# VectorE's expert additions and low halves put ahead of its other work in each slot of a MetaFormer block

## What is computed

```python
x = x + _L0_conv_ref(_ln_c(x), xl, qkv_w, proj_w, proj_b)   # super-token attention
t = _to_tokens(x)
t = t + _L0_ffn_ref(_ln_t(t), gate_w, gate_b, w1, b1, w2, b2)

# the first branch: 7 by 7 cells of 8 by 8 pixels, one super token each
aff = softmax(einsum('bnpc,bnck->bnpk', pix, sf9) * scale)   # pixel to 9 nearby cells
sft = fold3(einsum('bnpc,bnpk->bnck', pix, aff)) / aff_sum
q, k, v = split(qkv_w @ sft)                                 # 8 heads of 12
out = proj_w @ attention(q, k, v) + proj_b
pix_out = einsum('bnck,bnpk->bncp', unfold3(out), aff)

# the second branch: 4 experts, the best 2 of a softmax gate weigh the sum
h = gelu(einsum('bsd,edh->ebsh', x, w1) + b1)                # 96 -> 384
y = einsum('ebsh,ehd->ebsd', h, w2) + b2                     # 384 -> 96
out = einsum('bse,ebsd->bsd', masked, y)
```

## Time and profile before

| | |
|---|---|
| median of 3 runs | 509.77 us (508.06 to 514.8) |
| profiled execution | 509.76 us |
| its span, first to last instruction | 508.0 us |
| mean granted TensorE clock | 0.945 |
| busy share of the span: PE, DVE, ACT, POOL | 94%, 80%, 68%, 30% |
| PE line that starts each slot (L1345) | 100 times, from 81.1 to 501.7 us |

### The profile page before, as it was taken

How to read it: one execution, slowest core, us unless ns; L and a number is a source line. 1 busy time by engine, 2 the same in 40 slices (tenths; PEclk the granted TensorE clock), 3 DMA queues, 4 the chain that set the end, 5 groups by cost and what they waited for, 6 DMA issues and landing times.

```text
span 508.0 us, 14090 instructions
## 1 busy us (share of the span) xinstructions
PE 479.8 (94%) x5770; PEld 347.1 (68%) x5770; DVE 405.3 (80%) x1084; ACT 346.3 (68%) x333; POOL 154.8 (30%) x289
## 2 busy tenths in 40 slices
PE   9799879999899999899899999899899979999996
PEld 5797757776567777676566877676666657666665
DVE  6563875988899688988899687778799867888886
ACT  1026227578876849578877749669878938989883
POOL 3224012132870532131861541130343812112000
PEclk9759759999999999999899999899999989999999
DMA  8844015210120214210120210120220210223100
GB/s 237 286 141 144 1 33 132 43 34 17 32 56 19 48 34 112 50 32 17 33 56 18 48 34 19 32 48 17 32 57 17 49 33 21 47 48 79 26 17 20
DMA packets 55629, 28.18 MB, mean 55 GB/s; under 512 B 53534, under 2 KB 53670, under 8 KB 55173
## 3 DMA queue, kind: packets, MB, share of 16 engines
q1 hardware_dynamic: 54450, 24.99, 21.2%
q10 hardware_dynamic: 1114, 2.29, 1.4%
HBM read 12.33 MB, written 4.82 MB: 34 GB/s over the span
## 4 chain that ended last, share of the span: by engine, by line
PE 72%; DVE 8%; ACT 8%; issue 4%; DMA 4%; POOL 3%; SPq 0%; ACTq 0%; DVEq 0%; POOLq 0%
PE ps L1360 21%; PE ps L1388 16%; PE ps L1393 7%; PE ps L1380 5%; PE ps L1364 5%; PE ps L1223 4%; PE ps L1210 4%; ACT h L729 4%; DMA xt<-xtok 3%; ACT hh L737 2%; DVE xt L1068 2%; PE ps L1190 2%; PE ps L1300 2%; PE ps L1234 1%; PE ps L1345 1%
## 5 line engine op out<-in xcount | busy, mean ns | idle before, releaser
L729 ACT ACTIVATE h<-ps 128x1536 f32<-128x1536 f32 (+1 forms) x100 | 142.6, 1426 | 80.0 <-PE ps L1364 79.8
L1052 DVE TENSOR_TENSOR hl<-h,hh 128x1536 f16<-128x1536 f32 (+1 forms) x91 | 161.4, 1773 | 14.7 <-issue 13.7
L737 ACT CAST hh<-h 128x1536 f16<-128x1536 f32 (+1 forms) x91 | 133.3, 1465 | 2.9
L1068 DVE SCALAR_TENSOR_TENSOR xt<-ps,gl,xt 128x96 f32<-128x96 f32 (+1 forms) x400 | 99.8, 309 | 31.1 <-PE ps L1393 24.0
L510 POOL TENSOR_TENSOR x<-xs,x 128x384 f16<-128x384 f32 (+1 forms) x28 | 39.7, 1419 | 254.4 <-ACT x L693 254.4
L1388 PE MATMUL ps<-w_hi,hh 128*128 128x96 f16 x1092 | 107.2, 209 | 0.0
L1388 PE MATMUL ps<-w_lo,hh 128*128 128x96 f16 x1092 | 106.6, 209 | 0.0
L1388 PEld LDWEIGHTS ps<-w_hi,hh 128*128 128x128 f16 x1092 | 95.1, 100 | 10.0 <-issue 5.7
L1388 PEld LDWEIGHTS ps<-w_lo,hh 128*128 128x128 f16 x1092 | 96.2, 99 | 0.0
L1360 PE MATMUL ps<-xhl,w_a 128*128 128x512 f16 (+1 forms) x336 | 84.1, 360 | 3.1 <-DMA xhl<-x 3.1
L1360 PE MATMUL ps<-xhl,w_b 128*128 128x512 f16 (+1 forms) x336 | 82.8, 356 | 0.0
(11 more groups left out here) (168 smaller groups left out, 554.9 us busy)
## 6 DMA issues: line engine op xcount, KB each, us to landing
xch<-x SPq DMA_DIRECT2D x4, 1176.0 KB, 7.6
out<-xt SPq DMA_DIRECT2D x24, 192.0 KB, 2.2
xt<-xtok SPq DMA_DIRECT2D x4, 663.0 KB, 13.0
xt<-xtok SPq DMA_DIRECT2D x4, 612.0 KB, 11.3
h<-w ACTq DMA_DIRECT2D x2, 570.0 KB
h<-w ACTq DMA_DIRECT2D x1, 576.0 KB
xhl<-x SPq DMA_TRANSPOSE x28, 3.7
wqkv_sb<-wqkv ACTq DMA_DIRECT2D x1, 228.0 KB
```

What stands on the lines that cost most here:

```text
L729: act.activation(h32[:, i % 3, :, 0:width(i)], z, ACT.Gelu, scale=1.0 / WS).then_inc(S["h_ready"], 1)
L737: act.copy(hh[:, i % 3, :, 0:width(i)], h32[:, i % 3, :, 0:width(i)]).then_inc(S["hh_ready"], 1)
L1052: dve.tensor_tensor(hl[:, i % 2, :, 0:n], h32[:, i % 3, :, 0:n], hh[:, i % 3, :, 0:n], ALU.subtract).then_inc(S["hl_ready"], 1)
L1068: ins = dve.scalar_tensor_tensor(out=xt[0:n, b, t, 0:C], in0=ps[0:n, sum_bank(i), j * C:(j + 1) * C], scalar=gl[0:n, b % 2, t, e:e + 1], i ...
```

## The change

In each slot DVE now does the low part, the second side read and `add_expert(i)` first, and its normalising, statistics, sums and gates after it. Around that, numbers of slots are shifted:
- `NORMAL` becomes {2: 2, 5: 3, 8: 4, 10: 5, 12: 6}, and `unit_slots(b)` (17 or 16, 20) in place of (18 or 17, 20). `tokens_high`, `tokens_low` and `turn_tokens` of a unit come a slot later against the normalising than before.
- `affinity_sums` and `affinities_scaled` stand in slots 0 and 1 for images 1 and 2 (before: 1 and 2); in image 0 the sums stand in 0 and 1, the quotient in 1 and the scaling in 2.
- in slot 7 `attention_weights` comes first, then `add_expert(7)`, then `low_part(8)`.
- `gate_logits` moves from slot 21 to 22; the statistics of image b+2 are spread over other slots, and POOL's `deviation` goes from slot 8 to 9.
- on ACT, `hidden_high(i+2)` comes behind the side read that stood after it, and behind `attention_tanh`; the second copy of the projected heads (`projected_again`) is split off and done in slots 9 and 10.

No instruction is added or left out but the grouping of the statistics (100 in all as before).

```diff
-NORMAL = {0: 2, 4: 3, 8: 4, 10: 5, 12: 6}
+NORMAL = {2: 2, 5: 3, 8: 4, 10: 5, 12: 6}
...
         def unit_slots(b):
 
-            return pixels_over(b) + 1, 20
+            return pixels_over(b), 20
...
@@ sync @@
-                    if slot - 1 in NORMAL:
-                        turn_tokens(b, NORMAL[slot - 1])
+                    if slot - 2 in NORMAL:
+                        turn_tokens(b, NORMAL[slot - 2])
...
@@ gpsimd @@
-                    if slot in NORMAL:
-                        tokens_low(b, NORMAL[slot])
+                    if slot - 1 in NORMAL:
+                        tokens_low(b, NORMAL[slot - 1])
...
-                    if b + 2 < B and slot == 8:
+                    if b + 2 < B and slot == 9:
                         deviation(b + 2)
...
@@ scalar @@
                          ).then_inc(S["so_hi"], 1)
+
+            def projected_again(b, k):
+                rows = project_rows(k)
+                units = slice(rows[0], rows[-1] + 1)
                 act.wait_ge(S["so_hi"], 2 * b + k + 1)
                 act.copy(so[ZONE:2 * ZONE, units, :], so[0:ZONE, units, :]).then_inc(S["so_mid"], 1)
...
                 if i + 2 < ALL:
                     hidden_full(i + 2)
-                    hidden_high(i + 2)
                 after = divmod(i + 1, SLOTS) + (0,)
                 if i + 1 < ALL and read_at(*after):
                     side_read(read_at(*after))
-                if slot in NORMAL:
-                    tokens_high(b, NORMAL[slot])
+                if b + 1 < B and slot == 6:
+                    attention_tanh(b + 1)
+                if i + 2 < ALL:
+                    hidden_high(i + 2)
+                if slot - 1 in NORMAL:
+                    tokens_high(b, NORMAL[slot - 1])
                 if b + 1 < B:
                     if i == 0:
                         affinity_tanh()
                     if slot == 4:
                         affinities_high(b + 1)
-                    if slot == 6:
-                        attention_tanh(b + 1)
-                    if slot in unit_slots(b):
-                        tokens_high(b + 1, unit_slots(b).index(slot))
+                    if slot in (9, 10):
+                        projected_again(b + 1, slot - 9)
+                    if slot - 1 in unit_slots(b):
+                        tokens_high(b + 1, unit_slots(b).index(slot - 1))
...
@@ vector @@
-                if i + 1 < ALL:
+                late = slot == 7 and b + 1 < B
+                if late:
+                    attention_weights(b + 1)
+                elif i + 1 < ALL:
                     low_part(i + 1)
                 if second and READER[second[1]] == "dve":
                     side_read(second)
+                add_expert(i)
+                if late:
+                    low_part(i + 1)
                 if slot in NORMAL:
                     normalise(b, NORMAL[slot])
                 if b + 1 < B:
-                    if i == 1:
-                        affinity_quotient()
-                    if slot in (1, 2):
-                        affinity_sums(b + 1, slot - 1)
-                    if slot == 2:
+                    if b == 0 and slot < 2:
+                        if slot == 1:
+                            affinity_quotient()
+                        affinity_sums(1, slot)
+                    elif slot == 0:
+                        affinity_sums(b + 1, 0)
+                        affinity_sums(b + 1, 1)
+                    if slot == (2 if b == 0 else 1):
                         affinities_scaled(b + 1)
-                    if slot == 7:
-                        attention_weights(b + 1)
...
-                    if slot in (0, 3, 4, 5, 6):
-                        statistics(b + 2, *{0: (0, 4), 3: (4, 12), 4: (12, 16), 5: (16, 20), 6: (20, T)}[slot])
+                    if slot in (3, 4, 6, 7, 8):
+                        statistics(b + 2, *{3: (0, 7), 4: (7, 14), 6: (14, 18), 7: (18, 21), 8: (21, T)}[slot])
...
-                if b + 1 < B and slot == 21:
-                    gate_logits(b + 1)
-                add_expert(i)
+                if b + 1 < B:
+                    if slot == 22:
+                        gate_logits(b + 1)
```

More of the change, by code:

```diff
@@ L476, in _ @@
                 for slot in range(SLOTS):
-                    if slot - 1 in NORMAL:
-                        turn_tokens(b, NORMAL[slot - 1])
+                    if slot - 2 in NORMAL:
+                        turn_tokens(b, NORMAL[slot - 2])
                     if slot % E == 0 and slot > 0:
                         store(b, slot // E - 1)
-                    if b + 1 < B and slot - 1 in unit_slots(b):
-                        turn_tokens(b + 1, unit_slots(b).index(slot - 1))
+                    if b + 1 < B and slot - 2 in unit_slots(b):
+                        turn_tokens(b + 1, unit_slots(b).index(slot - 2))
                 store(b, UNITS - 1)
@@ L756, in _ @@
             heads_turned(0)
-            projected(0, 0)
-            projected(0, 1)
+            for k in range(2):
+                projected(0, k)
+                projected_again(0, k)
             for k in range(1, 4):
@@ L1153, in _ @@
                         normalise(b + 1, unit_slots(b).index(slot))
+                if b + 2 < B:
+                    if slot in (3, 4, 6, 7, 8):
+                        statistics(b + 2, *{3: (0, 7), 4: (7, 14), 6: (14, 18), 7: (18, 21), 8: (21, T)}[slot])
+                    if slot in (21, 22):
+                        affinity_shift(slot - 21)
+                if b + 1 < B:
+                    if slot == 22:
+                        gate_logits(b + 1)
                     if slot == 23:
```

5 lines of the change are left out of this document (1 added, 4 removed).

## The result

The changed kernel took 521.0 us (median, 519.87 to 522.83) where the kernel before took 510.24 beside it: a ratio of 1.0209, with a 95% interval of 1.0162 to 1.0256, so it is slower, and whether by more than 2% is left open. The forecast was 503.3, so the sign was wrong and the time lies beyond the range. The profiled execution took 519.87 us (span 518.1, clock 0.946), against 509.76 (508.0, 0.945): the 10.1 us to be explained stand within the span, and the mean clock is no worse.

What follows compares the result with a forecast made beforehand. PE's work (94% busy) was the floor, so only its waits could be won back. Terms -5.0 + 4.7 - 2.45 - 1.9 - 1.2 - 0.6 = -6.45 took 509.76 to 503.3 us; range 496 to 510.

Steps and rivals of the forecast that it cites:

- end of image 2: Gate logits behind slot 22's addition remove PE's 3.33 us wait and the half clock behind it: 5.0 us gained.
- image 0, slots 1 to 3: Scaled affinities come late, so SFT and slot 3 wait: 3.1 us lost, 4.7 with one half-clock stretch.
- images 1 and 2, slots 0 to 3: Sums and scaling a slot earlier, smaller waits, image 2 keeps its clock: 2.45 us gained together.
- slots 6 to 13 (heads late, then the gain): Images 0 to 2: 1.2 us lost each at the heads, slot 11's 1.8 wait gone: 1.9 us gained net.
- slots 14 to 18: Images 0 and 1: the prediction gave this stretch no term, so no loss or gain.
- image 3: Slots 4, 8 and 10: normalising moves into DVE's waiting time, so PE's waits of about 0.5 go: 1.2 us gained.
- slots 18 to 24 of images 0 and 1: Predicted for slots 22 to 24: 0.3 us gained in each image, 0.6 in all.
- The late heads: Slots 6 to 9, images 0 to 2: ACT's later high half delays PE's turning of the heads, 1.2 us lost each.
- one half-clock stretch of 1.6: Image 0's start: PE idles some 3 us in 4, so the clock falls once, adding 1.6 us to 3.1.
- Rival (b): Slots 6 to 13: ACT becomes the bound, high halves behind reads waiting for PE; 8.4 us lost, 511.7 us, chance 0.10.
- Its point of decision: The slower, ACT-bound case holds once the turning of the heads is later than 239.5 on the old clock.
- the later turned tokens: Put at nothing: ready two slots before the first layer wants them; without cover, each wait 1.5 to 4 us.

Runs made afterwards that it cites:

- run 7: Kernel before with the gate logits alone moved behind the addition of slot 22, instead of ahead of that of slot 21: 505.04 us, 0.9922 of the kernel before.
- run 4: Changed kernel with image 0's quotient, sums and scaling put ahead of the additions in slots 1 and 2, as before: 517.38 us, 1.0158 of the kernel before.
- runs 1, 3 and 6: Changed kernel with, respectively, ACT's hidden_high back behind hidden_full: 509.14 us; image 3's unit 2 normalised in slot 0: 518.19; DVE's pixel-bank read ahead of the low part: 511.33.
- Run 2: Kernel before with only ACT's order changed, hidden_high behind the side read and attention_tanh: 531.63 us, 1.0443 of the kernel before.
- run 6: Changed kernel, ACT's order as changed, but DVE reads the pixel bank (PIX) ahead of the low part: 511.33 us, 1.0033 of the kernel before.
- run 3: Changed kernel with unit 2 of image 3 normalised in slot 0, as before, instead of slot 2: 518.19 us, 1.0168 of the kernel before.
- Run 1: Changed kernel with ACT's hidden_high put back directly behind hidden_full, ahead of the side read and attention_tanh: 509.14 us, 0.9989 of the kernel before.

## Why the prediction was wrong

Its sum against the stretches of the table:

| step, as the prediction put it | predicted | measured |
|---|---|---|
| end of image 2 | -5.0 | -5.03 |
| image 0, slots 1 to 3 | +4.7 | +5.85 |
| images 1 and 2, slots 0 to 3 | -2.45 | -2.82 |
| slots 6 to 13 (heads late, then the gain) | -1.9 | +0.52 |
| slots 14 to 18 | no term | +8.98 |
| image 3 | -1.2 | +2.5 |
| slots 18 to 24 of images 0 and 1 | -0.6 | -0.56 |

**Right.** The end of image 2, both in size and in cause: run 7 moved the logits alone and gained 4.7. The starts of images 1 and 2. The fewer waits ahead of the additions in slots 18 to 24. The late heads, +1.34, +1.34 and +1.06 in slots 7 to 10 for a predicted 1.2 each: the turning of the heads starts 13.47 us behind the bias of slot 6 where it was 12.28, which is 1.2 later. One detail on the way was wrong and shows what was missed later on. PRT was to come 0.4 earlier; it came 0.7 later, since it waits in the bank for ACT's second read of AFT. PE's timeline:

```profile
124.74 0.61 PE L1280 MATMUL ps<-tab,prob 128*49 128x128 f32 x4 [0.97 <-ACT affT L649]
...
130.17 0.21 PE L1295 MATMUL ps<-tab,ao 49*96 49x49 f32 x1 [0.73 <-DVE ao L933]
```

The chain to the heads ended later than this wait, so the sum did not feel it.

**Image 0's start: the mechanism right, the clock's part open.** The waits came where they were predicted (SFT at 98.29, predicted 98.05; run 4 took the whole away). The sum had one half-clock stretch of 1.6. In the profiled execution the clock was at 0.50 for 6.8 us; in runs 1, 3 and 6, with the same order here and waits of 0.99 and 1.87 us, it was at 0.50 for 3.4 us, and the stretch took 23.70: +4.71, what was forecast. So the other 1.1 us are the clock's, and no run shows what decides on them.

**Slots 14 to 18: the step that failed.** The prediction's walk on ACT and DVE stopped at slot 13, and its sum has no term for slots 14 to 18 of images 0 and 1, which put them at nothing without a reason. Two links were left out. First, ACT's read of AFT, now ahead of the high half, is itself a wait for PE, so the copy inherits whatever makes PE late (in slots 7 to 9 this had been seen and costed). Second, `add_pixels`, which frees the bank, is not in the prediction at all. The earlier trace rows show ACT's read of AFT waiting for PE (0.57), and no row shows the second link, since in the kernel before the high half stood outside the ring. Runs 1 and 6 show both links: cutting either takes slots 14 to 18 from 20.64 back to 17.44 and 17.09 us in image 0. With the ring cut in run 6, 17.09, 17.09 and 12.27 us are left where the kernel before took 16.76, 16.76 and 11.44, so some 1.5 of the 8.98 us are not the ring's, and 0.93 are the clock's in image 0. Run 2 shows that ACT's order alone, put into the kernel before, is enough to make the ring. About 1 us of it per image stands already ahead of the bias of slot 14 (the 0.82 at 151.72, together with ACT's lateness), which is why "slots 6 to 13" gained nothing: with the ring cut (run 6), slots 10 to 14 took 15.48, 15.48 and 15.47 in images 0 to 2, 2.3 us under before on the mean.

**Rival (b)** named the mechanism on ACT ("the high halves stand behind reads that wait for PE") and the sign, but put it at the heads, gave 511.7, and a chance of 0.10. The heads did not pass their lateness on; the places with `add_pixels` did. Its point of decision (the turning later than 239.5; by the 1.2 above it came at 238.8 on that clock) said nothing on slots 14 to 18. It was argued down by "ACT is at 68% over all", a mean over stages: ACT sits still in the ring, so its share fell to 66% as it became the reason.

**Image 3: a second step that failed.** The prediction put at nothing "the later turned tokens (they are ready two slots before the first layer wants them". The cover was read in images 0 to 2. In image 3, with no side work, most slots take 3.25 us, and from the start of the normalising (441.58) over ACT, POOL and the DMA to PE's start (454.05) it is 12.5. The clause "without that cover each wait would be a transposing DMA of 1.5 to 4 us" had the size (3.58), and no rival used it. With a landing of 3.7 us, the median, in place of 5.6 the wait would have been some 1.7, by an estimate from these rows. Apart from the wait the additions gained most of the 1.2 predicted: with unit 2 early again (run 3) the image takes 0.86 us less than before.

## What to carry to other kernels

Before an instruction is put behind a read on an in-order engine, ask what that read waits for, and follow the chain until it closes or leaves the kernel: a buffer that is freed by another engine is a link like any other, and three short waits that form a ring cost their full time each turn, with no engine busy all the time (PE 4.0 of 5.4 us here). Walk every stage of the program in which the moved instruction occurs, not the one or two where the profile shows a wait now, and take the stage with the shortest steps to test a "ready long before". A change of many moves is worth splitting even where it loses: here three of its moves cost 21 us, and the others gained 10.

## What the hardware showed that was not expected

A wait of the same length did not do the same to TensorE's clock. The stretches of three kernels around the wait for the transposed tokens in image 3; length, busy PE, PEld, DVE, ACT, POOL, granted clock. The changed kernel first:

```profile
450.40:454.00 3.60, 0.07 (x2) 0.00 (x0) 3.60 (x10) 1.44 (x1) 0.00 (x0) 1.00 0.62 124
454.00:457.40 3.40, 3.35 (x47) 2.24 (x48) 0.21 (x1) 1.48 (x2) 0.00 (x0) 1.00 0.00 0
```

Run 4:

```profile
443.50:446.90 3.40, 1.38 (x33) 1.23 (x29) 3.40 (x10) 2.71 (x2) 0.00 (x0) 1.00 0.86 175
446.90:453.70 6.80, 5.30 (x37) 2.94 (x38) 1.72 (x2) 1.94 (x2) 0.00 (x0) 0.50 0.01 2
```

Run 1:

```profile
440.70:444.10 3.40, 3.40 (x14) 1.02 (x15) 1.59 (x1) 0.12 (x1) 0.00 (x0) 0.50 0.02 4
```

And the changed kernel in image 0:

```profile
97.30:104.10 6.80, 5.81 (x53) 5.82 (x54) 3.18 (x8) 1.54 (x2) 3.40 (x3) 0.50 0.27 51
```

PE sat 3.58 us in the changed kernel and the granted clock stayed at 1.00, the level of 2.4 GHz. It sat 3.52 us in run 4 at the same place, and the clock was at 0.50, 1.2 GHz, for 6.8 us, the start of which falls into the wait. It sat 2.11 in run 1 (the wait that ended at 440.67), and 3.4 us at 0.50 followed. The wait of run 4 in PE's timeline:

```profile
448.40 1.46 PE L1377 MATMUL ps<-xhl,w_a 128*128 128x512 f16 x3 [3.52 <-DMA xhl<-x]
```

In image 0 of the changed kernel the fall came while PE waited for the scaled affinities. The Trainium skill ("TensorE: Matmul & The Clock Gate", Part 1) has the gate follow how busy the engine has lately been; these rows agree that waiting is what comes first, and show that the length of a wait alone does not tell whether the clock falls. What tells the wait of 3.58 from that of 3.52 was not tried and is open. The clock moved 2.4 us between two kernels with the same order in this stretch (16.72 and 19.11 in slots 4 to 8 of image 3), so an edit's own gain is better read from its stretch than from the total.
